# Token rows turned by VectorE instead of TensorE, and six projections of each sample computed in that sample's own first quads

## The chip, the cores and the metric

One core of one Trainium2 chip runs the whole program. The metric is the device time of one execution in microseconds (us); lower is better.

## The reference, cut to what matters

A pre-norm cross-attention layer with sigmoid scores is followed by a mixture-of-experts feed-forward layer. The change touches only the first.

```
x, ctx: (8, 512, 256), (8, 1601, 256)        # 16 heads of 16, float32
q = layernorm(x) @ Wq.T * 0.25;  k = ctx @ Wk.T;  v = ctx @ Wv.T
s = sigmoid(einsum('blhd,bshd->bhls', q, k));  o = einsum('bhls,bshd->blhd', s, v)
x = x + o @ Wo.T
x = x + ffn(layernorm(x))     # router over 16 experts, each takes its best 64 tokens; a shared expert
```

## The kernel before

Stage A is the attention of the eight samples (called batches, b = 0 to 7), stage B the feed-forward layer. Stage A is written out by hand as a sequence of *quads*. A batch has 52 of them: four quarters of 13. A quarter (number 4b to 4b+3) is one half of the heads' dimensions (`half`) and one of two sets of rows (`e`); its quads q = 0 to 12 walk over the 1601 context positions in tiles of 128 (the last has 65). One quad is

- `scores(n)` on TensorE: two pairs of matmuls into the three `score` banks;
- two sigmoids on ScalarE (`probs`), 1024 columns each;
- `weighted_sum(n)` on TensorE, which adds probabilities times values into `acc`. The list `SUMS` lets it trail: a quad in which a projection is made gets no sum if only one is due, and the next quad makes two.

Between quads TensorE also makes the *products* (tasks) which the table `beside(b)` names by quad: ("K", b, half, chunk) keys of a 512-column context chunk (chunk 3 has 66 columns), ("V", b, chunk, two) values, ("Q", b, half) queries, ("T", b, k) four transposes that turn normalised token rows for the queries, ("O", b, t) the output projection and ("G", b) the router's logits. K, V, Q and O multiply high and low parts in three terms. All go through the one PSUM bank `misc`, so a product waits until VectorE has copied the one before it (`misc_copied`). Before the change every product of batch b+1 (six K of 512 columns, two of 66, seven V, two Q, two T) is made beside the quads of batch b; batch 0 also makes its own.

What follows a product, by queue:

- VectorE splits each result in two parts (`two_parts`) or copies it, makes both layer norms, adds up `acc` at each quarter's end (`acc_out`) and splits each context chunk (`split_ctx`) after the last task of the chunk before.
- SyncE's DMA queue writes keys to the DRAM scratch `key_scr` (`write_keys`), and `stack_keys(quarter)` reads them back with six DMAs into one of three `keys` buffers; `stack_queries` does so with twelve for the queries. Each waits for the landing of what it reads. In batch 0 alone, `place_keys` moves half 0's keys from SBUF to SBUF without the scratch.
- GpSimd's queue loads context chunks (`load_ctx`) and, per batch, places the 32x32 blocks of normalised attention output that VectorE has turned (`turn_norm`, `place_norm`, 16 DMAs, then `split_norm` on VectorE).

Stage B can start on TensorE once its first weights have been loaded by SyncE and split by GpSimd (`gu_hi`, `gu_lo`, `d_hi`, `d_lo`), which happens in batch 7.

## Time and profile before

| | us |
|---|---|
| median of 3 runs (lowest, highest) | 1366.72 (1365.53, 1369.01) |
| profiled execution, its own time | 1360.84 |
| its span, first to last instruction | 1359.0 |
| first sigmoid; end of the last one | 30.4; 941.2 |
| batch 0 (first sigmoid to batch 1's first) | 135.1 |
| a middle batch, 1 to 6 | 113.1 |
| batch 7 | 97.0 |

The span is read from the start of the first instruction; the profiled execution's own time has 1.8 us around it. TensorE's granted clock is full (1.00) in all of stage A. "Busy" TensorE counts modelled ends of pipelined matmuls: the distance from one row's start to the next one's start is what an operation takes of the engine.

### The profile page before, as it was taken

What the parts mean: (1) busy time and instruction counts of PE and PEld (TensorE: products, weight loads), DVE (VectorE), ACT (ScalarE), POOL (GpSimd) and SP (SyncE); (2) the same over time, 40 slices, a digit from 0 to 9 for tenths busy, and PEclk for the clock granted to TensorE, in tenths of its full rate; (3) what the DMA queues carried; (4) which work ended last, traced back from release to release, by engine and by line L of the source; (5) the groups of instructions that cost most, each with busy time, mean ns of one, the idle gap of its engine ahead of it and who ended that gap; (6) DMA issues with size and microseconds to landing.
All of it is one profiled execution on the core that took longest, in us unless ns stands there. A gap on an engine that the chain in (4) does not pass through costs nothing.

```text
span 1359.0 us, 22678 instructions
## 1 busy us (share of the span) xinstructions
PE 1323.2 (97%) x8882; PEld 760.3 (56%) x8882; DVE 632.4 (47%) x1257; ACT 982.4 (72%) x1145; POOL 286.4 (21%) x286
## 2 busy tenths in 40 slices
PE   4889999999999999999999999999999999999997
PEld 3444344444444444444444443324888888888887
DVE  4353254235326325423532631211657777777773
ACT  3568988888888888888888889998232445555553
POOL 1000011002002001100200200220000467777635
PEclk9999999999999999999999999999999999999999
DMA  6566774488389468558737936832533567777864
GB/s 155 143 136 160 124 158 137 113 132 210 104 127 186 149 105 172 147 110 133 208 103 130 184 118 80 154 128 87 178 124 124 180 174 187 195 187 187 195 124 47
DMA packets 119433, 196.85 MB, mean 145 GB/s; under 512 B 22752, under 2 KB 71904, under 8 KB 119328
## 3 DMA queue, kind: packets, MB, share of 16 engines
q1 hardware_dynamic: 99456, 161.44, 50.2%
q0 software_dynamic: 19584, 33.59, 12.5%
q8 instruction: 70, 1.15, 0.4%
q10 hardware_dynamic: 288, 0.39, 0.2%
q14 instruction: 35, 0.29, 0.1%
HBM read 118.99 MB, written 61.83 MB: 133 GB/s over the span
## 4 chain that ended last, share of the span: by engine, by line
PE 89%; ACT 5%; DVE 2%; issue 1%; SPq 1%; DMA 1%; POOL 0%; POOLq 0%; DVEq 0%; ACTq 0%
PE acc L1438 25%; PE score L1477 19%; PE score L1414 18%; PE score L1495 9%; PE misc L1322 6%; PE misc L1335 6%; ACT probs L742 5%; PE misc L1358 2%; PE misc L1343 2%; SPq L478 1%; PE misc L1350 1%; PE misc L1373 0%; POOL out L698 0%; DMA keys<-key_parts 0%; DMA xn<-x 0%
## 5 line engine op out<-in xcount | busy, mean ns | idle before, releaser
L742 ACT ACTIVATE probs<-score 128x1024 f32<-128x1024 f32 (+1 forms) x832 | 788.7, 1041 | 132.3 <-PE score L1414 126.2
L1438 PE MATMUL acc<-probs,values 128*32 128x512 f32 (+1 forms) x3328 | 412.5, 600 | 1.4 <-ACT probs L742 0.4
L1414 PE MATMUL score<-queries,keys 48*128 48x512 f32 (+1 forms) x1664 | 311.9, 449 | 3.6 <-DMA keys<-key_parts 2.6
L1414 PEld LDWEIGHTS score<-queries,keys 48*128 48x128 f32 (+1 forms) x1664 | 126.9, 180 | 260.5 <-ACT probs L742 200.2
L1438 PEld LDWEIGHTS acc<-probs,values 128*32 128x32 f32 (+1 forms) x3328 | 81.2, 109 | 181.2 <-issue 134.3
L625 POOL DMA_DIRECT2D ctx_raw<-ctx_t x32 | 23.4, 732 | 684.5 <-DVE ctx_lo L854 683.6
L752 ACT ACTIVATE gelu<-score 128x512 f32<-128x512 f32 (+1 forms) x100 | 57.3, 581 | 95.8 <-PE score L1477 94.1
L685 POOL DMA_INDIRECT gathered<-norm_scr,gather_row x64 | 81.3, 1270 | 202.6 <-DVE gather_row L1132 186.8
L1477 PE MATMUL score<-tok_hi,gu_hi 128*128 128x512 f32 (+1 forms) x400 | 120.8, 383 | 0.0
L1477 PE MATMUL score<-tok_lo,gu_hi 128*128 128x512 f32 (+1 forms) x400 | 120.1, 382 | 0.0
L1477 PE MATMUL score<-tok_hi,gu_lo 128*128 128x512 f32 (+1 forms) x400 | 120.1, 381 | 0.0
L698 POOL DMA_INDIRECT out<-result,add_row x64 | 108.5, 1695 | 47.8 <-ACT result L804 25.4
L890 DVE COPY values<-misc 128x512 f32<-128x512 f32 (+1 forms) x56 | 36.6, 653 | 171.0 <-PE misc L1335 171.0
L865 DVE CAST key_parts<-misc 128x512 fp32r<-128x512 f32 (+1 forms) x63 | 36.1, 574 | 168.1 <-PE misc L1322 168.1
L1079 DVE TENSOR_TENSOR hidden<-gelu,score 128x512 f32<-128x512 f32 (+1 forms) x100 | 66.1, 665 | 97.7 <-PE score L1477 68.5
L761 ACT ACTIVATE hid_hi<-hidden 128x512 fp32r<-128x512 f32 (+1 forms) x100 | 61.1, 613 | 58.6 <-DVE hidden L1079 56.2
L649 POOL DMA_DIRECT2D norm<-norm_blocks x112 | 59.9, 544 | 106.8 <-DMA resid_scr<-resid 104.9
L1477 PEld LDWEIGHTS score<-tok_lo,gu_hi 128*128 128x128 f32 x400 | 74.1, 188 | 14.6
L1477 PEld LDWEIGHTS score<-tok_hi,gu_lo 128*128 128x128 f32 x400 | 74.1, 188 | 14.6
L1477 PEld LDWEIGHTS score<-tok_hi,gu_hi 128*128 128x128 f32 x400 | 72.4, 189 | 13.3 <-issue 0.8
L804 ACT ACTIVATE result<-score,add_w 128x256 f32<-128x256 f32 x60 | 23.6, 474 | 68.0 <-DVE add_w L1122 64.9
L1086 DVE TENSOR_TENSOR hid_lo<-hidden,hid_hi 128x512 fp32r<-128x512 f32 (+1 forms) x100 | 66.5, 669 | 4.9 <-ACT hid_hi L761 0.3
(185 smaller groups left out, 1440.9 us busy)
## 6 DMA issues: line engine op xcount, KB each, us to landing
keys<-key_scr SPq DMA_DIRECT2D x180, 200.2 KB, 9.3
key_scr<-key_parts SPq DMA_DIRECT2D x45, 512.0 KB, 5.2
gu_raw<-w_gu SPq DMA_DIRECT2D x17, 1024.0 KB
ctx_raw<-ctx_t POOLq DMA_DIRECT2D x24, 512.0 KB, 4.3
queries<-query_scr SPq DMA_DIRECT2D x180, 64.0 KB, 2.8
d_raw<-w_d SPq DMA_DIRECT2D x17, 512.0 KB
query_scr<-query_parts SPq DMA_DIRECT2D x15, 512.0 KB, 4.8
norm<-xn SPq DMA_DIRECT2D x224, 32.0 KB
```

What stands on the lines that cost most here:

```text
L685: pool.indirect_dma_start(gathered[par][:, t, :], None, norm_scr[:, :], bass.IndirectOffsetOnAxis(ap=gather_row[par][:, t:t + 1], axis=0)) ...
L698: pool.indirect_dma_start(out[:, :], bass.IndirectOffsetOnAxis(ap=add_row[par][:, t:t + 1], axis=0), result[par][:, t, :], None, compute_o ...
L742: act.activation(probs[0:rows, n % RING, 2 * pair:2 * pair + 2, :], score[k % 3][0:rows, :, :], ACT.Sigmoid, scale=SCALE).then_inc(probs_d ...
L761: act.activation(hid_hi[par][:, of, cols], hidden[:, f % 2, cols], ACT.Copy).then_inc(hid_hi_done, 1)
L1079: dve.tensor_tensor(hidden[:, f % 2, cols], gelu[:, f % 2, cols], u_bank[:, f % 2, cols], ALU.mult).then_inc(hidden_done, 1)
L1086: dve.tensor_tensor(hid_lo[par][:, of, cols], hidden[:, f % 2, cols], hid_hi[par][:, of, cols].bitcast(F32), ALU.subtract).then_inc(hid_sp ...
L1322: mm = pe.matmul(bank[:, 0:n], W2[a][:, WK, k, P * half:P * (half + 1)], (ctx_hi, ctx_lo)[c][:, k, 0:n], start=(j == 0 and k == 0), stop=( ...
L1335: mm = pe.matmul(misc[0:n, D * i:D * (i + 1)], (ctx_hi, ctx_lo)[a][:, k, s0:s0 + n], W2[c][:, WV, k, :], start=(j == 0 and k == 0), stop=( ...
L1414: mm = pe.matmul(score[k % 3][0:rows, g, :], keys[quarter % KEY_RING][of, pair, P * st:P * st + rows], queries[half][of, e, pair, :], star ...
L1438: mm = pe.matmul(acc[32 * c:32 * (c + 1), :], values[b % 2][0:rows, st, half, c, :], probs[0:rows, n % RING, c, :], start=(st == 0), stop= ...
L1477: mm = pe.matmul(bank[:, f % 2, cols], (gu_hi, gu_lo)[a][slot][:, w, k, P * of:P * (of + 1)], (tok_hi, tok_lo)[b][par][:, k, cols], start= ...
L1495: mm = pe.matmul(d_bank[:, t2, D * (t % 2):D * (t % 2 + 1)], (hid_hi, hid_lo)[a][par][:, f, P * t:P * (t + 1)], (d_hi, d_lo)[b][slot][:, f ...
```

## The change

Four things change together.

1. The T products of batches 1 to 7 go. VectorE turns the blocks of `xn` (`turn_x`), GpSimd places them with 16 DMAs (`place_x`), and VectorE splits the result (`split_x`). The product Q(b, 0) waits for that (`x_split`).
2. V(b,2,1), K(b,1,2), K(b,0,3), V(b,3,0), Q(b,1) and K(b,1,3) of batches 1 to 7 are made in quads 0 to 13 of batch b itself, no longer beside batch b-1. The other eleven products of the next batch are spread over quads 17 to 48.
3. Chunks 2 and 3 of half 0's keys are placed from SBUF to SBUF in every batch (`late_keys`), so `stack_keys` reads only 1024 columns for half 0. TensorE waits for each late chunk at the first tile that needs it.
4. SyncE's queue is put in another order: half 1's queries and keys are stacked from quad 16 on, `load_x` and `store_norm` have other neighbours, and the first weights of stage B come behind ("G", 6), which is in quad 28 of batch 7 (it was quad 26).

```diff
     else:
-        tasks = {4: ("O", b - 1, 0), 7: ("O", b - 1, 1), 26: ("G", b - 1)}
-        at_quad = (0, 2, 10, 13, 15, 18, 21, 24, 28, 29, 31, 33, 35, 37, 39, 41, 43, 45, 47)
+        own = [("V", b, 2, 1), ("K", b, 1, 2), ("K", b, 0, 3), ("O", b - 1, 0), ("V", b, 3, 0), ("O", b - 1, 1),
+               ("Q", b, 1), ("K", b, 1, 3), ("G", b - 1)]
+        tasks = dict(zip((0, 2, 4, 6, 7, 9, 11, 13, 28), own))
+        at_quad = (17, 20, 23, 26, 31, 33, 36, 39, 41, 45, 48)
...
-                 ("T", c, 0), ("T", c, 1), ("Q", c, 0),
-                 ("K", c, 0, 2), ("K", c, 1, 2), ("V", c, 2, 0), ("V", c, 2, 1),
-                 ("K", c, 0, 3), ("K", c, 1, 3), ("V", c, 3, 0), ("Q", c, 1)]
+                 ("Q", c, 0), ("K", c, 0, 2), ("V", c, 2, 0)]
...
-DIRECT = [("K", 0, 0, kc) for kc in range(NCH)]
+LATE = range(2, NCH)
+DIRECT = [("K", b, 0, kc) for b in range(B) for kc in (LATE if b else range(NCH))]
...
+            def late_keys(b, kc):
+                sp.wait_ge(misc_copied, COUNT["K", b, 0, kc])
+                for e in range(2):
+                    sp.wait_ge(scores_done, GROUPS * (4 * b + e - KEY_RING + 1))
+                    place_keys(4 * b + e, kc, late_keys_in[e][kc - LATE[0]])
...
                     if q == 0 and b:
+                        stack_keys(4 * b + 1)
+                    if q == NST and b:
+                        store_norm(b - 1)
+                    if q == 16 and b:
                         stack_queries(b, 1)
                         stack_keys(4 * b + 2)
-                    if q == NST and b:
-                        store_norm(b - 1)
+                    if q == 22 and b:
                         stack_keys(4 * b + 3)
...
-                        if task == ("K", b + 1, 1, NCH - 1):
+                        if task == ("V", b + 1, 1, 1):
                             stack_keys(4 * b + 4)
-                            stack_keys(4 * b + 5)
+                        if task == ("V", b + 1, 2, 0) and b + 2 < B:
+                            load_x(b + 2)
...
+            for b in range(1, B - 1):
+                load_ctx(b + 1, 1)
+                load_ctx(b + 1, 2)
+                place_norm(b - 1)
+                load_ctx(b + 1, 3)
+                place_x(b + 1)
...
+            def turn_x(b):
+                dve.wait_ge(xn_ready, b + 1)
+                wait_past(dve, nt_stored, STORE * (b - 1))
+                turn_rows(xn, x_turned)
...
+                    if b + 1 < B and q == (21 if b == 0 else 28):
+                        turn_x(b + 1)
+                    if b + 1 < B and q == (31 if b == 0 else 35):
+                        split_x(b + 1)
```

Where instructions now stand, at three places. First TensorE in batch 0 from quad 19 on (`score` rows are `scores`, `acc` x8 are two weighted sums and x4 is one, `misc` rows are a product). Before:

```order
L1414 MATMUL score2<-queries0,keys1 128x512 x2
L1414 MATMUL score0<-queries0,keys1 128x512 x2
L1438 MATMUL acc<-probs,values0 32x512 x8
L1322 MATMUL misc<-ctx_hi,w_hi 128x512 x2
L1322 MATMUL misc<-ctx_lo,w_hi 128x512 x2
L1322 MATMUL misc<-ctx_hi,w_lo 128x512 x2
L1414 MATMUL score1<-queries0,keys1 128x512 x2
L1414 MATMUL score2<-queries0,keys1 128x512 x2
L1438 MATMUL acc<-probs,values0 32x512 x4
```

Now:

```order
L1479 MATMUL score2<-queries0,keys1 128x512 x2
L1479 MATMUL score0<-queries0,keys1 128x512 x2
L1501 MATMUL acc<-probs,values0 32x512 x8
L1479 MATMUL score1<-queries0,keys1 128x512 x2
L1479 MATMUL score2<-queries0,keys1 128x512 x2
L1501 MATMUL acc<-probs,values0 32x512 x4
L1479 MATMUL score0<-queries0,keys1 128x512 x2
L1479 MATMUL score1<-queries0,keys1 128x512 x2
L1501 MATMUL acc<-probs,values0 32x512 x4
```

The product K(1,0,1) has left the quad that makes two sums; it comes three quads later, in one that makes none.

Second, TensorE in batch 2 from quad 6 on. Before (quad 6 makes one sum, quad 7 O(1,1) and no sum):

```order
L1414 MATMUL score1<-queries0,keys2 128x512 x2
L1414 MATMUL score2<-queries0,keys2 128x512 x2
L1438 MATMUL acc<-probs,values0 32x512 x4
L1414 MATMUL score0<-queries0,keys2 128x512 x2
L1414 MATMUL score1<-queries0,keys2 128x512 x2
L1358 MATMUL misc<-w_hi,o_hi 128x256 x2
```

Now, from the last row of O(1,0) in quad 6 on:

```order
L1419 MATMUL misc<-w_hi,o_lo 128x256 x2
L1479 MATMUL score0<-queries0,keys2 128x512 x2
L1479 MATMUL score1<-queries0,keys2 128x512 x2
L1501 MATMUL acc<-probs,values0 32x512 x8
L1396 MATMUL misc<-w_hi,ctx_hi 65x256 x2
L1396 MATMUL misc<-w_lo,ctx_hi 65x256 x2
L1396 MATMUL misc<-w_hi,ctx_lo 65x256 x2
L1479 MATMUL score2<-queries0,keys2 128x512 x2
L1479 MATMUL score0<-queries0,keys2 128x512 x2
L1501 MATMUL acc<-probs,values0 32x512 x4
```

Quad 7 now has two sums and V(2,3,0), the only place in a middle batch where a quad has both.

Third, SyncE's DMA queue in batch 2, from its start to the stacking of quarter 10 (half 1, which TensorE reads from quad 26 on). Before, from the last DMAs of batch 1 on:

```order
L428 DMA query_scr01<-query_parts1 128x2x512
L437 DMA queries1<-query_scr01 16x1024 x12
L415 DMA keys1<-key_scr01 16x2x1602 x6
L403 DMA key_scr10<-key_parts0 128x2x512
L403 DMA key_scr11<-key_parts1 128x2x512
L453 DMA norm_scr<-norm 128x4x256
L455 DMA resid_scr<-resid 128x1024
```

Now:

```order
L422 DMA keys0<-key_scr00 16x2x1024 x6
L410 DMA key_scr01<-key_parts1 128x2x512
L490 DMA keys2<-key_parts0 16x2x66 x6
L490 DMA keys0<-key_parts0 16x2x66 x6
L437 DMA query_scr01<-query_parts1 128x2x512
L465 DMA norm_scr<-norm 128x4x256
L467 DMA resid_scr<-resid 128x1024
L410 DMA key_scr01<-key_parts1 128x2x66
L446 DMA queries1<-query_scr01 16x1024 x12
L422 DMA keys1<-key_scr01 16x2x1602 x6
```

The queries and the full-width keys of half 1 (the last two rows) were the first reads of the batch; now they stand behind the half's last product, two stores and two groups of six placements.

## Rows read from the trace of the kernel before

**Rows 1.** Busy time of TensorE by stretch: batch 1, batch 3, batch 7, batch 0.
```profile
core 0: us, PE busy (x), PEclk, DMA share, GB/s
165.53:278.68 113.15, 113.15 (x811) 1.00 0.62 136
391.71:504.88 113.17, 113.17 (x811) 1.00 0.69 147
844.18:941.16 96.98, 95.61 (x668) 1.00 0.47 105
30.40:165.53 135.13, 125.87 (x853) 1.00 0.64 142
```
**Rows 2.** Timeline of TensorE, batch 3 (start and duration in us, then what runs).
```profile
395.53 0.73 PE L1414 MATMUL score<-queries,keys 48*128 48x512 f32 x4
396.19 0.72 PE L1322 MATMUL misc<-ctx_hi,w_hi 128*128 128x512 f32 x2
...
397.78 0.73 PE L1414 MATMUL score<-queries,keys 48*128 48x512 f32 x4
398.44 1.93 PE L1438 MATMUL acc<-probs,values 128*32 128x512 f32 x16
400.30 0.74 PE L1414 MATMUL score<-queries,keys 48*128 48x512 f32 x4
...
452.89 0.66 PE L1350 MATMUL misc<-ident,xn 128*128 128x128 f32 x4
453.48 0.87 PE L1414 MATMUL score<-queries,keys 48*128 48x512 f32 x4
...
482.82 0.41 PE L1322 MATMUL misc<-ctx_hi,w_hi 128*128 128x66 f32 x2
...
483.61 0.73 PE L1414 MATMUL score<-queries,keys 48*128 48x512 f32 x4
...
490.77 0.45 PE L1335 MATMUL misc<-w_hi,ctx_hi 128*65 128x256 f32 x2
...
491.62 0.73 PE L1414 MATMUL score<-queries,keys 48*128 48x512 f32 x4
```
**Rows 3.** Timeline of ScalarE, batch 7 (in brackets its idle time before).
```profile
855.85 3.77 ACT L742 ACTIVATE probs<-score 128x1024 f32<-128x1024 f32 x4 [0.57 <-PE score L1414]
...
862.32 34.69 ACT L742 ACTIVATE probs<-score 128x1024 f32<-128x1024 f32 x38 [0.59 <-PE score L1414]
```
**Rows 4.** Timeline of ScalarE, batch 0: quad 20, quad 34.
```profile
94.99 5.84 ACT L742 ACTIVATE probs<-score 128x1024 f32<-128x1024 f32 x6 [2.44 <-PE score L1414]
...
128.27 5.85 ACT L742 ACTIVATE probs<-score 128x1024 f32<-128x1024 f32 x6 [2.15 <-PE score L1414]
```
**Rows 5.** DMA issues of the page: operation, count, KB each, median us to landing.
```profile
keys<-key_scr SPq DMA_DIRECT2D x180, 200.2 KB, 9.3
...
norm_t_scr<-nt_lo SPq DMA_DIRECT2D x8, 512.0 KB, 4.0
...
norm<-norm_blocks POOLq DMA_DIRECT2D x112, 32.0 KB, 6.3
```
**Rows 6.** Landing of L415's DMAs, then of L649's, with the extremes.
```profile
DMA to landing us min/median/max: 4.1/9.3/18.2
...
DMA to landing us min/median/max: 3.0/6.3/8.8
```
**Rows 7.** Timeline of SyncE's and GpSimd's queues, batch 3.
```profile
401.97 5.42 SPq L437 DMA_DIRECT2D queries<-query_scr  x12
407.50 3.72 SPq L415 DMA_DIRECT2D keys<-key_scr  x6
...
427.60 8.62 POOL L649 DMA_DIRECT2D norm<-norm_blocks  x16 [2.11 <-DMA resid_scr<-resid]
```
**Rows 8.** VectorE, batch 3: layer norm beside the placing; copy, turn and split.
```profile
417.58 1.25 DVE L972 STREAM_TRANSPOSE norm_blocks<-norm 128x1024 f32<-128x1024 f32 x1
...
434.53 1.37 DVE L933 TENSOR_SCALAR xn<-xn,mv,rs 128x256 f32<-128x256 f32 x4
439.54 0.69 DVE L890 COPY values<-misc 128x512 f32<-128x512 f32 x1 [3.63 <-PE misc L1335]
440.51 0.43 DVE L981 CAST nt_hi<-norm 128x512 fp32r<-128x512 f32 x1 [0.28 <-DMA norm<-norm_blocks]
...
442.04 0.69 DVE L983 TENSOR_TENSOR nt_lo<-norm,nt_hi 128x512 fp32r<-128x512 f32 x1
```
**Rows 9.** The placing DMAs of L649: shortest, median and longest issue in ns.
```profile
L649 POOL DMA_DIRECT2D norm<-norm_blocks x112: 539/539/654, 199.3 to 882.5; - x112
```
**Rows 10.** Timeline of GpSimd, batch 7: stage B's first weights.
```profile
912.47 2.39 POOL L664 TENSOR_TENSOR d_lo<-d_raw,d_hi 128x1024 fp32r<-128x1024 f32 x1
```

More of the change, by code:

```diff
@@ L324, in build @@
         norm_ready = sem("norm_ready")
+        x_turned = sem("x_turned")
+        x_placed = sem("x_placed")
+        x_split = sem("x_split")
         norm_turned = sem("norm_turned")
@@ L332, in build @@
         first_keys_in = [sem(f"first_keys_in{i}") for i in range(NCH)]
+        late_keys_in = [[sem(f"late_keys_in{e}{kc}") for kc in LATE] for e in range(2)]
         keys_in = [sem(f"keys_in{i}") for i in range(KEY_RING)]
@@ L421, in stack_keys @@
                 b, half, _, _ = quad_of(NST * quarter)
-                keys_written(("K", b, half, NCH - 1))
+                late = b and half == 0
+                keys_written(("K", b, half, LATE[0] - 1 if late else NCH - 1))
                 wait_past(sp, scores_done, GROUPS * (quarter - KEY_RING + 1))
-                read_keys(quarter, 0, TP, keys_in[quarter % KEY_RING])
+                read_keys(quarter, 0, CHUNK * LATE[0] if late else TP, keys_in[quarter % KEY_RING])
             def write_queries(b, half):
@@ L447, in load_x @@
             def load_x(b):
-                sp.wait_ge(misc_copied, COUNT["T", b - 1, KC - 1])
+                if b == 1:
+                    sp.wait_ge(misc_copied, COUNT["T", 0, KC - 1])
+                else:
+                    sp.wait_ge(x_split, b - 1)
                 sp.dma_start(xn[:], x_rows[b]).then_inc(x_in, 16)
@@ L478, in place_keys @@
                         sp.dma_start(
-                            keys[quarter][stack_rows(j, g), :, s0:s0 + n].bitcast(F32),
+                            keys[quarter % KEY_RING][stack_rows(j, g), :, s0:s0 + n].bitcast(F32),
                             key_parts[buf][scratch_rows(e, g), part, 0:n].bitcast(F32)
@@ L549, in load_resid @@
                 sp.dma_start(resid_in[b % 2][:], resid_scr[b]).then_inc(resid_read[b % 2], 16)
-            sp.wait_ge(misc_copied, COUNT["V", B - 1, NCH - 1, 0])
+            sp.wait_ge(misc_copied, COUNT["G", B - 2])
             keys_written(KEY_ORDER[-1])
+            for e in range(2):
+                for arrived in late_keys_in[e]:
+                    sp.wait_ge(arrived, STACK_DMAS * (B - 1))
             for half in range(2):
@@ L642, in _, with place_blocks @@
                 load_ctx(0, kc)
+            def place_blocks(to, placed_one):
+                for i in range(BLOCKS):
+                    for j in range(BLOCKS):
+                        pool.dma_start(to[TURN * j:TURN * (j + 1), :, P * i:P * (i + 1)],
+                                       norm_blocks[TURN * i:TURN * (i + 1), j::BLOCKS, :]).then_inc(placed_one, 16)
             def place_norm(b):
@@ L646, in place_norm, with place_x @@
                 pool.wait_ge(norm_turned, b + 1)
[L647 to L656 removed]
+                place_blocks(tok_raw, norm_placed)
+            def place_x(b):
+                pool.wait_ge(x_turned, b)
+                place_blocks(x_raw, x_placed)
+            for kc in range(NCH):
+                load_ctx(1, kc)
+            place_x(1)
+            load_ctx(2, 0)
+            for b in range(1, B - 1):
[4 more added lines that the diff above has]
+                place_x(b + 1)
+                if b + 2 < B:
+                    load_ctx(b + 2, 0)
             place_norm(B - 2)
@@ L874, in key_chunk @@
                 if i >= 2 and KEY_ORDER[i - 2] in DIRECT:
-                    before = KEY_ORDER[i - 2][3]
-                    dve.wait_ge(first_keys_in[before], STACK_DMAS)
-                    dve.wait_ge(keys_in[1], STACK_DMAS * (before + 1))
+                    _, of, _, before = KEY_ORDER[i - 2]
+                    if of:
+                        for e in range(2):
+                            dve.wait_ge(late_keys_in[e][before - LATE[0]], STACK_DMAS * of)
+                    else:
+                        dve.wait_ge(first_keys_in[before], STACK_DMAS)
+                        dve.wait_ge(keys_in[1], STACK_DMAS * (before + 1))
                 else:
@@ L983, in split_norm, with split_x @@
                     last = dve.tensor_tensor(lo, raw, hi.bitcast(F32), ALU.subtract)
-                last.then_inc(norm_split, 1)
+                last.then_inc(split_one, 1)
+            def split_norm(b):
+                dve.wait_ge(norm_placed, PLACE_DMAS * (b + 1))
+                split_rows(tok_raw, norm_split)
+            def split_x(b):
+                dve.wait_ge(x_placed, PLACE_DMAS * b)
+                split_rows(x_raw, x_split)
             def gate_logits(b):
@@ L1386, in product @@
                 elif kind == "Q":
+                    if task[2] == 0:
+                        wait_past(pe, x_split, b)
                     mm = query_product(task[2], bank)
@@ L1406, in scores @@
                     pe.wait_ge(keys_in[quarter % KEY_RING], keys_loaded(quarter))
+                if b and half == 0 and st % (CHUNK // P) == 0 and P * st // CHUNK in LATE:
+                    pe.wait_ge(late_keys_in[e][P * st // CHUNK - LATE[0]], STACK_DMAS * b)
                 if st == 0 and (e == 0 or quarter == 1):
```

45 lines of the change are left out of this document (17 added, 28 removed).

## The prediction

> **What bounds the kernel now.** I read the stretches first: attention takes 30.4 to 941.2 us of the span of 1359.0, and only there does the change move work. In [rows 1] TensorE is busy for all of a middle batch (113.15 of 113.15 us), at full clock, and for 95.61 of 96.98 us in batch 7. But a busy TensorE may only be waiting inside pipelined matmuls, so I next took the distances from start to start in its timeline. In [rows 2] the four score matmuls of a quad take 396.19 - 395.53 = 0.66 us, a 512-column key product 397.78 - 396.19 = 1.59, and the sums of two quads 400.30 - 398.44 = 1.86, so 0.93 each. A quad alone therefore costs TensorE 0.67 + 0.93 = 1.60 us. ScalarE needs more: in [rows 3] 38 sigmoids without a break take 34.69 us, 0.91 each, 1.82 per quad. So a quad without a product leaves TensorE 0.22 us to spare, and a full product of 1.60 us takes up the spare time of seven quads.
>
> A middle batch has 52 quads and, in the order before, 16 full products (six K, six V, two Q, two O), two K of 66 columns (483.61 - 482.82 = 0.79 us), one V of 65 rows (491.62 - 490.77 = 0.85) and two T (453.48 - 452.89 = 0.59 each), all from [rows 2], and the router's product. 52 x 1.60 + 16 x 1.60 + 1.58 + 0.85 + 1.18 = 112.4, and with about 0.6 for the router 113.0. The batch takes 113.1 [rows 1]. That is the main reading: **the middle batches go at TensorE's pace, with no idle time to win.** ScalarE's pace would be 52 x 1.82 = 94.6 us. Batch 7 takes 97.0, 2.4 more, for it has two O and the router only. Batch 0 takes 135.1: TensorE is idle for 9.3 us of it, and where a product and two sums share a quad ScalarE stands still for 2.44 and 2.15 us [rows 4], against 0.57 for one product without a sum [rows 3].
>
> **The change, part by part.** Seven pairs of T go, one in each of batches 0 to 6; each frees TensorE of 1.18 us. In batches 1 to 6 the six moved products leave for the batch before and come in from the batch after, so TensorE's work falls by the T alone. The gaps between products there become at most four quads: four quads and a product are 4 x 1.60 + 1.60 = 8.0 us for TensorE and 7.3 for ScalarE, so TensorE remains the one that sets the pace. Only the 66-column K in quad 13, four quads before the next, lets it fall idle, for about 0.1. Quad 7 with two sums and the small V piles up work, but TensorE is late there anyway; in the worst case it costs what such a quad costs beyond the rest, some 0.4. I take 1.1 us saved per batch, **6.6 us in six** (bounds 0.7 and 1.2, that is 4 to 7).
>
> *Batch 0* keeps its first thirteen quads and loses eight of the nineteen products for batch 1 behind them: three full products, three small ones and two T, together 4.8 + 2.4 + 1.2 = 8.4 us of TensorE. How much of that is time? Quads 20 to 51 now last from 94.99 [rows 4] to 165.5, 70.5 us, where ScalarE's pace is 32 x 1.82 = 58.2; with the 2.44 us before them, 14.7 us are lost from quad 19 on. Afterwards full products stand there at quads 22, 25, 28, 32, 37, 43 and 48. A product d quads before the next costs 1.60 - 0.22 d where TensorE catches up late (0.94, 0.94, 0.72), and never under a gap of 0.57 and 0.1 to get going again [rows 3]: 2.6 + 4 x 0.7 = 5.4, and 0.7 for the two sums of quad 19 behind the product in 18. So 14.7 - 6.1 = **8.6 us saved**. Bounds: no less than 4, if two gaps of 2.2 us come back at another place; no more than 10.
>
> *Batch 7* takes the six products. TensorE's work in quads 0 to 14 is 15 x 1.60 + 5 x 1.60 (V, K, Q and the two O) + 1.58 + 0.85 = 34.4 us, ScalarE's 15 x 1.82 = 27.3: 7.1 us lost, and 0.3 at the router's product, against 2.4 before. **5.0 us lost** (bounds 4 and 6); behind quad 14 TensorE has its 0.22 us per quad to spare, but ScalarE cannot win back what it lost.
>
> *VectorE* turns xn in 1.25 us and splits it in 442.04 + 0.69 - 440.51 = 2.2 us [rows 8], where it split two transposed tiles before (four instructions as well); it stands waiting for TensorE ahead of its copies (3.63 us at 439.54, [rows 8]), so I cost it at nothing. *GpSimd* has 16 more DMAs per batch, 8.6 us [rows 7], and nothing else to do. *SyncE* issues 24 placements per batch in place of keys read at full width. The weights of stage B are ready at 912.5 + 2.4 = 914.9 us [rows 10] and needed at 942; two quads later is 4 us. Hidden. What these three hide has a condition each, which the rivals take up.
>
> Sum: -8.6 - 6.6 + 5.0 = **-10.2 us**. The profiled execution's own time is 1360.84 (1.8 around its span), so 1350.6 for such a one; the median of the runs shown is 1366.72, 5.9 higher, so 1356.5. With every bound on one side it is -13 or -2; the forecast's own range is -13 to -7, so 1353.7 to 1359.7.
>
> **A rule weighed.** In batch 3 VectorE normalises xn from SBUF to SBUF at 434.53 [rows 8], in the middle of the sixteen placing DMAs of 427.60 to 436.22 [rows 7], and of all 112 of these the longest took 654 ns to issue where the median is 539 [rows 9]. The sum keeps 8.6 us for sixteen. The Trainium skill speaks against the way the rows are placed: in SBUF — State Buffer, section "SBUF: two separate sides", a DMA issued by GpSimd cannot write its descriptors while VectorE runs a two-port copy, and one of 620 ns took 3100 ns beside such a copy. By that figure sixteen would take some 50 us, an estimate from the page, TensorE would wait for the queries in every batch, and the kernel would be over 100 us slower. The rows above do not agree with it here.
>
> **Rivals.** *Half 1's keys come late (slower).* With TensorE's distances, counted from the batch's start: Q(b,1) in quad 11 is copied at 29.3 us, the norm is ready at 30.7 (1.4 us of layer norm, [rows 8]), the last K is copied at 32.4 and written. Behind the two stores the twelve query reads issue until 38.2 and the six key reads until 41.9 (5.4 and 3.7 us, [rows 7]). With the median landing of 9.3 us [rows 5] they are there at 51.2. TensorE starts quad 26 at 26 x 1.60 + 8 x 1.60 + 2.4 = 56.8. So 5.6 us are spare. But the longest landing was 18.2 [rows 6], when reads queued behind reads: then 60.1, 3.3 us late in each of seven batches, +23, and the result is 1380. At 1.5 us late per batch (landing after 16.4 us) the whole gain is gone. For it: stores of 1 MB, a context chunk and sixteen placements are in flight at that time. Against: the queries' issue gives the queue 5 us to drain. Chance 0.12 that it costs over 1 us a batch.
>
> *The turned rows come late (gain halved).* Turning starts after the router's product in quad 28, at 63.5, is through at 64.8, placed at 73.4 (8.6), landed at 79.7 by the median of 6.3 [rows 5] and 82.2 at the longest [rows 6]. Until then VectorE stands at the split, with V(c,1,0) of quad 36 behind it, so split and copy end at 82.6 to 85.1. V(c,1,1) in quad 39 needs that at 39 x 1.60 + 12 x 1.60 + 3.7 = 85.3. Spare 2.7 or 0.2. The turning waits for the store of the previous rows, which lands at about 60 (4.0 us, [rows 5]) unless the keys of quarter 4b+3 hold it up; 3 us more and each batch loses 1 to 3 us, 6 to 18 in six: 1360 to 1370. Chance 0.1.
>
> *Batch 0 gives only part.* Its gaps may come from VectorE, where a context chunk's split precedes a product, and not from two sums with a product; then 4 us instead of 8.6: 1361. Chance 0.14.
>
> *The turning gives nothing.* Eight transposes take TensorE 1.18 us per batch, the new way takes 1.25 us of VectorE and 8.6 us of DMA issue [rows 2, 7, 8], so taken alone it is the longer one. If all that the T rows free is lost again in waits for `x_split`, the seven batches lose 7 x 1.2 = 8.3 us of the gain and the result is 1364.8. Against it: TensorE is the full engine [rows 1], and a result that is 2.7 us early costs it nothing. Chance 0.03. The Trainium skill (VectorE: DVE Perf Modes, "Rules for kernel authors") would choose the old way: 128x128 on TensorE where PSUM will do as the destination.
>
> **How the numbers follow.** Forecast 0.58, -13 to -7. Keys late 0.12, of it 0.07 slower than before. Turned rows late 0.1. Batch 0 in part 0.14. The turning gives nothing 0.03. Other waits that I do not see 0.03. A measurement of this kernel tells 0.3% (4.1 us) from no change. Forecast and batch 0 in part are faster by more, and half of the turned rows: 0.78. Within it 0.12, slower 0.10. The range 1351 to 1366 leaves out the worse half of the late cases above and little below.
>
> **What would show it.** The busy rows of the changed kernel: middle batches of 112 us with TensorE still busy throughout, batch 0 of 126 to 127, batch 7 of 102. ScalarE's timeline: no gap over 2 us after quad 19 of batch 0; in batch 7 gaps up to quad 15 and none after but at the router's. A wait of the score matmuls for `keys` at a quarter's start, or of `misc` products for VectorE behind `xn`, would be the rivals. I am wrong if a middle batch is not shorter by about 1 us, since TensorE's load is the whole argument.

## The result, and the profile after

| | before | after |
|---|---|---|
| median of 20 runs each (lowest, highest) | 1365.03 (1359.69, 1369.01) | 1369.82 (1357.49, 1383.27) |
| ratio after to before, 95% interval | | 1.004 (1.0024 to 1.0055) |
| profiled execution; its span | 1360.84; 1359.0 | 1376.86; 1375.0 |
| first sigmoid; end of the last one | 30.4; 941.2 | 29.9; 957.2 |
| batch 0 | 135.1 | 131.3 |
| batches 1 to 6 | 113.1 each | 112.4, 116.9, 112.9, 112.4, 113.6, 119.3 |
| batch 7 | 97.0 | 108.5 |

The changed kernel is 0.4% slower; 0.7% faster was forecast. The ratio and its interval leave out the four of the twenty runs that lie more than 1.5% above the fastest (1380.5 to 1383.3); with them the ratio of the means is 1.005. All of the 16.0 us between the two profiled spans lies ahead of the end of the last sigmoid, so stage B is as it was. The fastest run is at 1357.5, near the 1356.5 that was forecast for the median: something is lost in most executions, and not the same each time. The profiled execution is one of the longer ones, 7 us above the median.

The busy rows of TensorE that answer to [rows 1] (batch 1, batch 2, batch 6, batch 7, batch 0):

```profile
core 0: us, PE busy (x), PEclk, DMA share, GB/s
161.18:273.58 112.40, 112.10 (x804) 1.00 0.53 135
273.58:390.46 116.88, 113.66 (x804) 0.99 0.62 138
710.50:829.70 119.20, 113.93 (x806) 0.97 0.59 132
848.60:957.20 108.60, 104.79 (x710) 0.95 0.49 101
29.91:161.18 131.27, 119.06 (x804) 0.99 0.56 133
```

Batch 1 is what was forecast (112.0). In batches 0, 2, 6 and 7 TensorE has more idle time than before, and its granted clock is below 1.00, which in [rows 1] it never was. The waits of VectorE and of TensorE name what came late:

```profile
DVE nt_hi L1032 <- DMA xn<-norm_blocks: 46.5, 6, 11.7
...
DVE norm_blocks L1015 <- DMA norm_t_scr<-nt_lo: 20.9, 5, 5.1
```
```profile
PE misc L1396 <- DVE values L933: 10.4, 5, 4.9
PE score L1479 <- DMA keys<-key_parts: 5.5, 3, 3.6
PE score L1479 <- DMA keys<-key_scr: 3.0, 1, 3.0
```

(us in total, times, longest.) Three places, one for each of TensorE's rows.

**Quad 39 of batches 2, 3, 5 and 6.** The distance from the first sigmoid of one quad to that of the next is here 5.54, 2.67, 3.37 and 8.66 us, and in batches 1 and 4 it is 2.06. VectorE in batch 2, which began at 273.58:

```profile
330.48 0.43 DVE L1032 CAST nt_hi<-norm 128x512 fp32r<-128x512 f32 x1 [3.97 <-DMA norm<-norm_blocks]
...
342.19 1.25 DVE L1015 STREAM_TRANSPOSE norm_blocks<-xn 128x1024 f32<-128x1024 f32 x1 [4.86 <-DMA norm_t_scr<-nt_lo]
...
358.46 0.43 DVE L1032 CAST nt_hi<-xn 128x512 fp32r<-128x512 f32 x1 [9.69 <-DMA xn<-norm_blocks]
...
360.59 0.68 DVE L933 COPY values<-misc 128x512 f32<-128x512 f32 x1
```

and the queues of SyncE and GpSimd beside it:

```profile
312.00 3.74 SPq L422 DMA_DIRECT2D keys<-key_scr  x6
...
321.38 3.75 SPq L422 DMA_DIRECT2D keys<-key_scr  x6
...
333.11 0.43 SPq L475 DMA_DIRECT2D norm_t_scr<-nt_lo  x1
...
349.27 3.94 SPq L422 DMA_DIRECT2D keys<-key_scr  x6
```
```profile
309.00 8.51 POOL L672 DMA_DIRECT2D norm<-norm_blocks  x16 [0.95 <-DMA resid_scr<-resid]
...
343.74 8.50 POOL L672 DMA_DIRECT2D xn<-norm_blocks  x16 [7.56 <-DVE norm_blocks L1015]
```

Read as a chain: the norm's placings (309.0) and the twelve key reads (312.0, 321.4) are in flight together, and the placings have landed at 330.5. Store of the split norm 333.1, landed 342.1. Turning 342.2, placing 343.7 to 352.2, beside the next key reads (349.3), landed 358.4. While VectorE waits for that, the copy of V(c,1,0), made in quad 36, stands behind the split; it runs at 360.6, and TensorE can begin V(c,1,1) only then:

```profile
361.33 0.50 PE L1396 MATMUL misc<-w_hi,ctx_hi 128*128 128x256 f32 x2 [2.90 <-DVE values L933]
```
```profile
355.00:362.00 7.00, 4.09 (x33) 1.45 (x26) 2.75 (x5) 4.82 (x6) 0.00 (x0) 1.00 0.36 52
362.00:366.00 4.00, 4.00 (x25) 1.81 (x27) 2.52 (x3) 1.94 (x2) 0.00 (x0) 0.58 0.00 0
366.00:380.00 14.00, 14.00 (x98) 5.38 (x92) 3.52 (x5) 11.39 (x12) 0.73 (x1) 1.00 0.36 110
```

The second view has PE, PEld, DVE, ACT and POOL in this order, then the granted clock. After a stretch in which TensorE was busy for 4.09 of 7.00 us the clock is granted at 0.58 for 4 us, most of it at the lower level (1.2 GHz), then full again. Quads 39 and 40 of batch 2 take 9.1 us where batch 1 needs 4.6: 4.5 us, of which 2.9 are TensorE's idle time.

Batches 3 and 6 have something more. GpSimd in batch 6:

```profile
798.77 1.60 POOL L672 DMA_DIRECT2D xn<-norm_blocks  x3 [7.23 <-DVE norm_blocks L1015]
802.80 6.91 POOL L672 DMA_DIRECT2D xn<-norm_blocks  x13 [2.43 <-issue]
```

After the third placing it issues nothing for 2.4 us; in batch 3 it issues nothing for 1.7 us after the twelfth. Both pauses are in every profiled execution in which VectorE turns x, at the same placings and of the same length to 0.03 us. So batch 6 turned 0.8 us earlier than batch 2 and landed 2.0 us later, and batch 3, without its pause, would have landed at 80.8 instead of 82.5. The profile gives no reason for them.

**Quad 26 of batch 7.** SyncE, GpSimd and TensorE, then the stretches of the batch (PE busy, clock):

```profile
880.69 6.30 SPq L446 DMA_DIRECT2D queries<-query_scr  x12
887.10 7.56 SPq L422 DMA_DIRECT2D keys<-key_scr  x12
```
```profile
883.21 8.50 POOL L672 DMA_DIRECT2D norm<-norm_blocks  x16 [73.50 <-DMA resid_scr<-resid]
```
```profile
904.78 0.72 PE L1479 MATMUL score<-queries,keys 48*128 48x512 f32 x4 [2.96 <-DMA keys<-key_scr]
```
```profile
848.60:898.60 50.00, 49.70 (x354) 1.00 0.55 102
898.60:920.00 21.40, 18.44 (x114) 0.76 0.96 196
920.00:957.20 37.20, 36.65 (x248) 1.00 0.12 46
```

The batch began at 848.6. The first six key reads (quarter 30) are issued 38.5 to 41.6 us into it and have landed at 56.1; TensorE stands ready at 53.2. After the 3 us of idle time the clock averages 0.76 over 21 us (about 10 of them at the lower level), in which the DMA engines are 96% busy.

**Quads 11 to 13 of batch 0**, which the change doesn't touch. ScalarE at the first sigmoids of quads 13 and 14, after and before:

```profile
75.73 1.94 ACT L781 ACTIVATE probs<-score 128x1024 f32<-128x1024 f32 x2 [3.97 <-PE score L1479]
81.48 1.94 ACT L781 ACTIVATE probs<-score 128x1024 f32<-128x1024 f32 x2 [3.81 <-PE score L1479]
```
```profile
73.25 1.94 ACT L742 ACTIVATE probs<-score 128x1024 f32<-128x1024 f32 x2 [1.97 <-PE score L1414]
77.36 1.94 ACT L742 ACTIVATE probs<-score 128x1024 f32<-128x1024 f32 x2 [2.17 <-PE score L1414]
```

Together 4.3 us later in the profiled execution after the change.

### The profile page after: what moved, and what is told of

The parts are those of the page before. It is cut to its first block, busy times and chain, and to the rows that moved or that the text cites. A ratio compares the mean times of both kernels' runs of the same rounds, so it can differ in the third digit from the quotient of the medians.

```text
span 1375.0 us, 22918 instructions
## 1 busy us (share of the span) xinstructions
PE 1322.5 (96%) x8826; PEld 753.7 (55%) x8826; DVE 635.1 (46%) x1264; ACT 982.7 (71%) x1145; POOL 346.3 (25%) x398
## 3 DMA queue, kind: packets, MB, share of 16 engines
q0 software_dynamic: 23168, 37.27, 13.7%
## 4 chain that ended last, share of the span: by engine, by line
PE 69%; DMA 11%; DVE 6%; POOL 5%; issue 4%; ACT 3%; SPq 2%; POOLq 0%; DVEq 0%; ACTq 0%
PE score L1540 19%; PE acc L1501 17%; PE score L1479 11%; PE score L1558 9%; PE misc L1396 5%; PE misc L1383 4%; DMA norm<-norm_blocks 4%; DMA norm_t_scr<-nt_lo 3%; ACT probs L781 3%; POOL norm L672 2%; POOL xn L672 2%; DMA xn<-norm_blocks 2%; PE misc L1419 2%; DMA resid_scr<-resid 1%; DMA keys<-key_scr 1%
## 5 line engine op out<-in xcount | busy, mean ns | idle before, releaser
L1501 PE MATMUL acc<-probs,values 128*32 128x512 f32 (+1 forms) x3328 | 420.1, 607 | 3.4 <-DVE o_sum L989 2.5
L1501 PEld LDWEIGHTS acc<-probs,values 128*32 128x32 f32 (+1 forms) x3328 | 80.6, 109 | 187.9 <-issue 133.0
L800 ACT ACTIVATE hid_hi<-hidden 128x512 fp32r<-128x512 f32 (+1 forms) x100 | 61.1, 613 | 58.6 <-DVE hidden L1140 56.8
L843 ACT ACTIVATE result<-score,add_w 128x256 f32<-128x256 f32 x60 | 23.7, 476 | 67.9 <-DVE add_w L1183 64.7
L672 POOL DMA_DIRECT2D xn<-norm_blocks x112 | 59.6, 540 | 45.8 <-DVE norm_blocks L1015 41.7
## 6 DMA issues: line engine op xcount, KB each, us to landing
keys<-key_scr SPq DMA_DIRECT2D x96, 200.2 KB, 11.2
```

The lines of the kernel that those rows point to most:

```text
L672: pool.dma_start(to[TURN * j:TURN * (j + 1), :, P * i:P * (i + 1)], norm_blocks[TURN * i:TURN * (i + 1), j::BLOCKS, :]).then_inc(placed_on ...
L800: act.activation(hid_hi[par][:, of, cols], hidden[:, f % 2, cols], ACT.Copy).then_inc(hid_hi_done, 1)
L1501: mm = pe.matmul(acc[32 * c:32 * (c + 1), :], values[b % 2][0:rows, st, half, c, :], probs[0:rows, n % RING, c, :], start=(st == 0), stop= ...
```

## The experiments

All are edits of the changed kernel but one. Ratios are to the kernel before, on the same chip. "Into the batch" counts from the batch's first sigmoid.

**1. The turned rows go to another place (own_blocks).**

```diff
+        x_blocks = norm[:].rearrange("p t d -> p (t d)").rearrange("p (j c) -> p j c", c=P)
             def turn_x(b):
                 dve.wait_ge(xn_ready, b + 1)
-                wait_past(dve, nt_stored, STORE * (b - 1))
-                turn_rows(xn, x_turned)
+                turn_rows(xn, x_turned, x_blocks)
             def split_x(b):
                 dve.wait_ge(x_placed, PLACE_DMAS * b)
+                wait_past(dve, nt_stored, STORE * (b - 1))
```

> Edit: xn is turned into the space of the normalised rows (dead from the norm's split to the next layer norm), so the turning no longer waits for the store of nt_lo; that wait stands before the split instead. Theory (the turned rows are late because their chain starts 2.6 to 5.1 us late behind nt_stored): VectorE's gap ahead of the turning falls under 1 us, the last placement lands 3 to 5 us earlier in batches 2 to 6, quads 39 of batches 2, 3, 5 and 6 no longer stand out, each middle batch takes 112.4 to 113 us, and 13 us of the changed kernel's profiled span come back (1375.0 to about 1362). Rival (the sixteen placements are slow because SyncE's key reads share the DMA engines with them): the placements are issued earlier but take longer, the last landing moves by less than 1 us, and quads of 3 to 8 us stay at 39. Rival 2: the stall only moves, to Q(c,0) in quad 41 or to the split that now waits for the store.

Measured: median 1361.1, ratio 0.998 (0.9961 to 0.9999); one of its twelve executions took 7044 us, which nothing here explains. Span 1359.1. Batches 2, 6 and 7:

```profile
274.66:386.93 112.27, 111.96 (x804) 1.00 0.63 144
723.82:836.00 112.18, 111.86 (x804) 1.00 0.58 138
836.00:941.40 105.40, 101.87 (x710) 0.98 0.50 105
```

The placing in batch 2 starts 339.39 - 274.66 = 64.7 us into the batch, where the changed kernel had 343.74 - 273.58 = 70.2, and lands at 74.4 instead of 84.9. No quad of a middle batch stands out, and the stall has not moved to another place. In batches 2 to 6 the last landing comes 6.3 to 10.5 us earlier, not 3 to 5: in most batches the placings are now issued by 73.4, before SyncE's next key reads begin at 75.6 to 75.8, so they land faster too. So this run doesn't decide between a late start and reads beside the placings; experiment 3 does. Of the 15.9 us that the profiled span falls by, 13.7 are in the middle batches. Another 3.2 are in batch 7, which the edit doesn't touch: TensorE waits 2.7 us there instead of 3.0, and the low clock behind the wait is shorter.

**2. The split one quad later (split36).**

```diff
-                    if b + 1 < B and q == (31 if b == 0 else 35):
+                    if b + 1 < B and q == (31 if b == 0 else 36):
                         split_x(b + 1)
```

> Edit: VectorE splits the placed rows of x one quad later, behind the copy of V(c,1,0), and not ahead of it. Theory (PE waits at quad 39 for a copy that is queued on VectorE behind the wait for the placements): the placements may land 87 us into a batch instead of 82.4, the stalls of 4.5 and 6.9 us in batches 2 and 6 of the changed kernel go (landings were at 84.9 and 86.9), middle batches take 112.4 to 113, the span falls by 10 to 13 us. Rival: Q(c,0) in quad 41 needs the split in any case, and the stall moves there with the same size: no change in the batch times.

Median 1359.3, ratio 0.9977 (0.9961 to 0.9993), span 1361.0. Middle batches 112.2 to 112.3; the placings start 65 to 68 us into the batch and land at 76 to 85. Only batch 6's (84.8) is later than the changed order bears, and there quad 39 takes 2.06 us, where a landing at 84.9 cost the changed kernel 4.5. The stall doesn't move to Q(c,0). Batch 7 is 109.3.

**3. SyncE's key reads held back (hold_keys, one execution).** `stack_keys(4b + 4)` waits for `x_placed`.

> Edit of the changed kernel alone: SyncE reads the next batch's first keys only when the placements of x have landed. Theory of contention (the sixteen placements land late because SyncE's reads share the DMA engines): in batches 2 to 6 the last placement lands within 4 us of its issue instead of 6 to 7, landings come 2 to 4 us earlier in the batch (after 79 to 83 us instead of 82 to 87), and the quads at 39 lose less than 1 us. Theory of the chain (the placing starts late): the issue of the last placement stays at 75 to 80 us into the batch and a quad of over 3 us at 39 remains in at least one of batches 2 to 6. Batch 7 and batch 0 as in the changed kernel, 105 to 109 and 128 to 132.

Time 1357.3, span 1355.5. Landings of the sixteen placings of batch 2, the changed kernel, then this one:

```profile
DMA to landing us min/median/max: 1.7/2.5/6.7
```
```profile
DMA to landing us min/median/max: 1.7/2.1/3.1
```

The last placing of a batch lands 1.7 to 3.0 us after its issue, in the changed kernel 4.5 to 7.1 in batches 2 to 6. They have all landed by 81.9. Contention's forecast holds. But the placings start as late as before (65 to 71 us) and, against the chain's forecast, no quad 39 is longer than the 2.06 us of an undisturbed one by more than 0.1. So a stall takes both, a late start and a slow landing: with the reads held, the late start alone costs nothing, here for one execution. Experiment 1, with its early start, keeps most placings clear of the reads as well.

**4. TensorE turns the rows again, the moved products stay (t_back).** T(c,0) and T(c,1) in quads 35 and 37, no `turn_x`, `place_x`, `split_x`.

> Edit: the turning by VectorE is undone and the moved products stay: T(c,0) and T(c,1) are TensorE transposes again, in quads 35 and 37 (33 and 35 in batch 0), with no placements of x and no split. Theory (turning is worth 1.2 us of TensorE per batch when nothing is late, and its chain is what costs in batches 2, 3, 5 and 6): no quad over 3 us at 36 to 41, every middle batch 113.5 to 114 us, batch 7 as in the changed kernel (about 102 or 108), profiled span 1375.0 - 13 + 8 = about 1370 with batch 7 at 108, median 1364 to 1368. Rival (the late quads have nothing to do with x's chain, but with the place of the values' copies or SyncE's reads): stalls of several us stay, and the time is 5 to 8 us above the changed kernel's.

Median 1372.5, ratio 1.0064 (1.004 to 1.0088), span 1370.7. Batch 2:

```profile
275.83:389.63 113.80, 113.29 (x812) 1.00 0.59 139
```

No late quad in the middle batches, which take 113.6 to 113.8; batch 7 is 107.5. The median is 4.5 us above the band given. Beside experiment 1, where turning is not late either, its middle batches are 1.4 us longer (113.6 to 113.8 against 112.2 to 112.4): that is what turning by VectorE is worth per batch once it is in time, a little more than TensorE's 1.18 for the two T. Quad 36, between the two T, takes 3.7 us, so some of that is their place. The medians are 11.4 us apart; of the 11.6 us between the profiled spans 8.6 are in the middle batches, and 2.1 in batch 7, which has no turning in either. Against the changed kernel, with its stalls, nothing is decided: the two ratios to the kernel before, 1.0064 and 1.004, have intervals that overlap.

**5. The kernel before again (before_again, one execution).**

> The kernel before once more, unchanged, to see how much of its own first batch differs between executions. Theory (quads 11 to 13 of batch 0, whose code the change doesn't touch, are lost or kept by the landing of one key placement, in both kernels): batch 0 is 135 us or 139 us, the others 113.1 and 97.0 as before; where it is 139, quads 12 and 13 take near 5.9 and 5.7 us. Rival (those quads are slower only in the changed kernel): batch 0 is 135 again.

Time 1365.5, span 1363.6, and batch 0 is 140.7. ScalarE at quads 13 and 14:

```profile
75.51 1.94 ACT L742 ACTIVATE probs<-score 128x1024 f32<-128x1024 f32 x2 [3.97 <-PE score L1414]
81.24 1.94 ACT L742 ACTIVATE probs<-score 128x1024 f32<-128x1024 f32 x2 [3.79 <-PE score L1414]
```

The same two rows as in the changed kernel: the wait belongs to both kernels. It is 4.2 of the 5.5 us by which this batch 0 is longer than in the first profiled execution. What goes with it shows in the landing of the last of the twelve placements of half 0's keys that SyncE issues from about 64 us on; after (a kernel with the wait), then before:

```profile
DMA to landing us min/median/max: 3.8/3.8/3.8
```
```profile
DMA to landing us min/median/max: 1.8/1.8/1.8
```

In all six profiled executions with the wait, of any kernel here, that placement is issued 0.3 to 0.5 us after GpSimd's issue of a context load and takes 3.8 to 4.1 us to land; in all seven without it, 0.05 to 0.07 us before that load, and it takes 1.8. The two go together in thirteen of thirteen, but no run moves the load, so a cause isn't shown. How many of the unprofiled executions have the wait can't be read directly; of 24 runs of the kernel before, 18 had a mean clock of 0.997 or less, like this one (0.996), and took 1362.1 to 1366.7 us, and six had 0.998 or 0.999, like the first profiled one, and took 1358.1 to 1362.6.

**6. The changed kernel again (again, one execution).**

> The changed kernel once more, unchanged. Theory (its stalls at quad 39 hang on landings at 82 us into the batch, which vary): middle batches of 112.3 to 120 us with late ones in other batches or of other sizes than 4.5, 0.5, 1.2 and 6.9 us; batch 7 again 105 to 114, for quad 26's keys are late in every execution. Rival (stalls set by the order of instructions alone): the same four batches and the same sizes to 0.3 us.

Time 1367.0. Batches 1 to 7: 112.3, 117.8, 112.4, 113.8, 113.1, 112.3, 108.2. The late quads 39 are those of batches 2, 4 and 5 (6.2, 3.6, 2.8 us), in the first profiled run those of 2, 3, 5 and 6. Landings at 80.6 to 81.4 cost nothing, at 82.7, 83.4 and 84.5 they cost 0.8, 1.5 and 5.5 us. Batch 0 is 126.95, with no wait at quads 11 to 13.

**7. Batch 7's queue in another order (b7_order).**

```diff
-                    if q == NST and b:
+                    if q == NST and b and b + 1 < B:
                         store_norm(b - 1)
                     if q == 16 and b:
                         stack_queries(b, 1)
                         stack_keys(4 * b + 2)
+                        if b + 1 == B:
+                            store_norm(b - 1)
                     if q == 22 and b:
+                        if b + 1 == B:
+                            sp.wait_ge(scores_done, 2 * (QPB * b + 24))
                         stack_keys(4 * b + 3)
```

> Edit, batch 7 only: the norm is stored behind the reads of queries and of quarter 30, and the reads of quarter 31 wait until quad 24's scores are done. Theory (quad 26 comes at 49.6 us into batch 7 and not at 56.8, and the reads of quarter 30 land up to 3 us after it, beside two 512 KB stores and the reads of quarter 31; then the granted clock is at half for 10 us): batch 7 falls from 108.5 to 101.6 to 103 us. Rival (the slow landing is that of the issue order on SyncE, twelve query reads ahead of six key reads): the key reads land within 1 us of the time before, batch 7 stays over 106. Middle batches as in the changed kernel, with their stalls at quad 39 in whichever batch they fall.

Median 1380.7, ratio 1.0139 (1.0113 to 1.0166): a miss (its profiled execution, at 1373.9, is the shortest of five). Quad 26 is on time, its keys have landed 50.4 us into the batch, so the rival of the issue order falls, but the norm is stored later, so it is placed later, and the router's product in quad 28 waits:

```profile
906.59 1.08 PE L1438 MATMUL misc<-norm,gate 128*32 128x128 f32 x16 [8.10 <-DMA norm<-norm_blocks]
```

Batch 7 takes 113.6. (The next expectation gives this wait as 9.8 us: that is the length of the whole quad.) Batch 6 had its turned rows late too (quad 39: 9.3 us).

**8. The same, with the router's product later (b7_late).** Experiments 1 and 7, and in batch 7 `split_norm` at quad 31 and ("G", 6) in quad 34.

> Edits: x turned into the dead space of the norm (as in own_blocks), and in batch 7 the norm stored behind the reads of quarter 30, quarter 31's reads held until quad 24, and, because that alone made the router's product wait 9.8 us, the norm's split moved to quad 31 and the router's product to quad 34. Theory: batch 7 takes 101.6 to 102.5 us with no quad over 2.5 us after quad 15, middle batches 112.3, batch 0 128 to 133, profiled span 1352 to 1357, median 3 to 5 us under own_blocks' 1361. Rival (the norm's placings then land beside quarter 31's reads, and either the split at quad 31 or quad 39's keys are late): a quad of over 3 us at 28 to 40 and batch 7 over 104. Rival 2: weights for stage B are issued 10 us later and the first product of stage B waits, so the span stays at 1359.

Median 1354.8, **ratio 0.9929 (0.9904 to 0.9954)**, span 1350.5. Batches 0, 1 and 7:

```profile
28.50:156.47 127.97, 118.83 (x804) 0.99 0.59 137
156.47:268.80 112.33, 112.03 (x804) 1.00 0.56 135
830.25:932.15 101.90, 100.60 (x710) 1.00 0.47 109
```

The batches are as the theory had them. The median is 6.3 us under experiment 1 (3 to 5 were given), and the span lies 1.5 us under its band, for batch 0 has no wait at quads 11 to 13 in this execution and had one in experiment 1's (132.6). Stage B hardly waits for its weights: the span falls by 8.6 us beside experiment 1, the end of the last sigmoid by 9.2.

**9. Both (all4).** Experiments 2 and 8.

> As b7_late, and the split of x behind the copy of V(c,1,0) (one quad later). Theory: with the turning no longer late, the split's place is worth nothing in most executions; within 1 us of b7_late, smaller spread at most. Rival: landings beyond 82 us still happen in some executions of b7_late, and this one is 1 to 3 us faster in the median. Against the kernel before: 0.993 to 0.996.

Median 1358.1, ratio 0.9939 (0.9917 to 0.9961). Middle batches 112.2 to 112.5 and batch 7 101.9, as in 8; in its profiled execution batch 0 has the wait at quads 11 to 13 (131.6). Its median is 3.3 us above that of 8, where 1 us at most was given, but the intervals of 8 and 9 overlap, and the batches differ only by that wait: the split's place is worth nothing that shows once the turning is early.

**10 and 11. Which traffic delays quarter 30's keys (b7_hold31, b7_store).** Both on experiment 1. The first holds only quarter 31's reads; the second only moves the norm's store behind quarter 30's reads, with the split at quad 31 and the router's product in quad 34.

> Edit on own_blocks: in batch 7 only the reads of quarter 31 are held until quad 24's scores are done; the norm's store and placings stay where they are. Theory A (quarter 30's reads are slowed by the reads of quarter 31 issued right behind them): the last key of quarter 30 lands 3 us or more earlier than at 55.8 us into the batch, quad 25 stays under 2 us, batch 7 is 101.9 to 102.5. Theory B (they are slowed by the norm's placings and its store, which run beside them): landing stays within 1.5 us of 55.8, a quad of 3 us or more remains at 25, batch 7 is 104 to 106.

> Edit on own_blocks: in batch 7 the norm is stored behind the reads of quarter 30 (so its placings start later), split at quad 31, router's product at quad 34; the reads of quarter 31 are not held. Theory B: quarter 30's last key lands at 46 to 48 us into the batch, batch 7 is 101.9 to 102.5. Theory A: quarter 30's last key still lands after 52, and quad 25 takes over 3 us. If both this one and the one that only holds quarter 31 come to 102, either share of the traffic is enough.

Landings of quarter 30's six reads, and who waited for them, 10 and then 11:

```profile
  PE score L1482: 2.3, 1
...
DMA to landing us min/median/max: 6.7/9.1/13.9
```
```profile
DMA to landing us min/median/max: 4.3/6.8/9.1
```

Number 10: the last key lands at 55.5 us into the batch, as before (55.8); batch 7 104.9; ratio 0.9994 (0.9973 to 1.0015). Number 11: it lands at 50.2 (46 to 48 was given); batch 7 101.9; ratio 0.9945 (0.9926 to 0.9964), median 1357.1. Theory B: it is the norm's traffic, its two stores and sixteen placings, that holds the keys up, and not the reads behind them.

## Why the prediction was wrong, step by step

**Right: TensorE's load.** A middle batch was to be 112.0; undisturbed it is 112.3 (0.8 us saved, 1.1 forecast). The 0.3 us are idle time that no middle batch had before: 34.4 us into each, a weighted sum waits for VectorE's `o_sum`. Batch 0 was to be 126 to 127: it is 126.7 to 128.1 in five executions of the new order without the wait at quads 11 to 13, and 130.0 in a sixth, which lost 3 us at quads 1 and 2. Batch 7 was to be 102: it is 101.9 once its keys are in time. With all three in place (experiment 8) the kernel is 0.7% faster, which is the size that was forecast (10.2 of 1366.7 is 0.75%), but for a kernel with the further edits named there.

**Wrong: "Hidden", for VectorE, GpSimd and SyncE.** The sum gave the queues' work no price, and put the conditions under the rivals with 0.12 and 0.10. This is the step that failed. The first rival came true in batch 7, in each of the seven profiled executions of an order with the norm's store still ahead of the reads; the second in some of batches 2 to 6, in both profiled executions of the changed kernel. The mechanisms were right, the times in them too short and so the chances too small.

- *The turned rows come late.* The store of the norm's parts was to land "at about 60" by a median of 4.0 us. It is issued at 55.5 to 59.5 and lands at 62.4 to 68.5, 6.9 to 10.4 us after its issue, so turning began up to 5.1 us later than the 63.5 reckoned, and the placings landed at 81.4 to 86.9 in batches 2 to 6, where 79.7 to 82.2 was forecast from 63.5. The sixteen placings were taken at 8.6 us in every batch; with the pauses they are 10.2 in batch 3 and 10.9 in batch 6. The latest landing that the forecast allowed, 82.4 (85.3 less 2.9 for split and copy), stood (of the 3.7 us in 85.3, small products and the router account for 3.0; measured, V(c,1,1) starts at 84.9 in batch 1): landings at 74.6 and 81.4 cost nothing, 82.5 cost 0.5 us, 83.1 cost 1.2, 84.9 cost 4.5 and 86.9 cost 6.8. Together 13.1 us in the profiled execution, in the range of "6 to 18 in six" that the rival gave.
- *Half 1's keys come late.* Two errors. The landing was taken at the median of before, 9.3 us; it is 14.5, at 56.1 instead of 51.2. And "TensorE starts quad 26 at 56.8" was used for all batches. It holds for the middle ones, where TensorE starts it at 56.3. The keys are there by 52.3 to 55.5, so nobody waits, but 0.8 us are to spare in two of them and not 5.6; in batch 4 of experiment 11 they landed at 56.3, just as TensorE came. But batch 7 has no products behind quad 13 to slow it, and there TensorE is at quad 26 at 53.2. The spare 5.6 us are -2.9, and with the low clock behind them batch 7 takes 6.6 us more than 101.9.
- *What neither had:* after the longer waits the granted clock fell to its lower level (1.2 GHz), so that a wait costs more than its own length. TensorE's waits of 0.6 and 1.2 us (batches 3 and 5) were not followed by it; 2.9 us in batch 2 cost 4.5, 5.0 us in batch 6 cost 6.8. How much is added isn't set by the wait. In seven profiled executions TensorE stood for 2.0 to 3.0 us before quad 26 of batch 7: in two of them (experiments 1 and 10) the low clock lasted 3.4 us, and the batch took 3.5 and 3.0 us more than 101.9; in five it lasted 10.2 or 13.7 us, and the batch took 5.6 to 7.4 us more.

The profiled execution lies 26.2 us above its forecast at the last sigmoid: 13.1 at the quads 39, 6.6 in batch 7, 4.3 at batch 0's quads 11 to 13, and 2 to 3 in the six middle batches at 0.3 to 0.4 each, less than a us elsewhere. The 4.3 are in one of two profiled executions of the kernel before as well; in the forecast of the median they are probably part of the 5.9 us between that profiled execution and the median. Experiment 6, nearer the changed kernel's median, lies 15.7 us above: 7.8 at the quads 39, 6.3 in batch 7 and 1.6 elsewhere.

**The rival "the turning gives nothing"** asked for the gain of 8.3 us to be lost in waits. In the profiled execution of the changed kernel 13.1 us were, though not by TensorE's own wait for the queries' rows but through the copy behind the split. What falls is that turning is worth nothing in itself (experiments 1 and 4). The Trainium skill's choice of TensorE for a 128x128 transpose (VectorE: DVE Perf Modes, "Rules for kernel authors") is not borne out in this kernel, where TensorE is the full engine: the old way costs 1.4 us more per middle batch. *Batch 0 gives only part* falls: in those five it gave 7.0 to 8.4 of 8.6. The chances of a result faster by more than 0.3% add up to 0.77, not 0.78.

The Trainium skill has a rule that bears on the term missing from the sum, in Trainium Kernel Development and Optimization, section "Key Constraints": DMAs from the queues of SyncE, ScalarE and GpSimd run on the same 16 engines and interleave, and a second queue saves only issue time. Experiments 3, 10 and 11 agree that the queues delay each other: the slowest of SyncE's six reads lands after 9.1 us when the norm's stores and placings are not beside them and after 13.9 when they are, and the slowest placing after 3.1 us without reads beside it and 6.7 with them.

Still open: whether the context load is what makes the placement of batch 0's keys late (no experiment touched it), what GpSimd's pauses are, what decides how long the low clock lasts, and the share of the stores against the placings in what delays quarter 30's keys, since experiment 11 moved both.

## What to carry to other kernels

Work that leaves the full engine for a chain of DMAs costs nothing only while the chain is in time: write down for each hand-over when it is needed in each stage apart, the last stage too, where fewer products make the consumer faster. Price landings at the spread seen when the queues overlap as they will after the change, not at the median of before. And before taking a chain apart, look for the one wait in it that exists only because of a shared buffer: here the use of a dead 512 KB tile let the placings of batch 2 start 5.5 us earlier and land 10.5 us earlier, for no cost. And before calling a difference an edit's, look at the stages that it doesn't touch: batch 7 took 105.4 or 108.5 us mostly by the length of the low clock.

## What the runs showed of the hardware

- GpSimd's 224 placing DMAs kept their issue time of 539 ns (at most 569), the 100 that ran beside an instruction of VectorE as well as the rest; the slowest stood beside the layer norm's step from SBUF to SBUF. So the blocking of GpSimd's DMAs that the prediction weighed (the Trainium skill, SBUF — State Buffer, "SBUF: two separate sides") doesn't show here either:

```profile
L672 POOL DMA_DIRECT2D xn<-norm_blocks x112: 539/539/560, 102.6 to 809.2; - x112
L672 POOL DMA_DIRECT2D norm<-norm_blocks x112: 539/539/569, 195.7 to 891.2; - x112
```

- SyncE's reads of 200 KB landed after 11.2 us at the median (9.3 in [rows 5]) though there were only 96 of them for 180; what else was in flight with them had changed.
- Between two such issues GpSimd can pause by itself: 1.7 us in batch 3 and 2.4 us in batch 6 while x is placed, in all ten profiled executions that place x, and 1.8 us in batch 6 while the norm is placed, in both of the kernel before. In batch 6 of the changed kernel's first profiled execution VectorE ran nothing in that time.
- In batches 1 to 7, waits of TensorE of 2.0 us and more were followed by 3.4 to 13.7 us of lower granted clock: the clock is 0.58 over 4 us in batch 2 and 0.76 over 21 us in batch 7. In the kernel of experiment 8, whose middle batches and batch 7 have no such wait, the clock is 1.00 in them.
